# Attention stage: GpSimd multiplies one of four value rows, and its gathers are issued behind both sums of a pair

## The reference

```
gather = seg_id[:, :, None] - offsets            # 4 rows per token
scores = jnp.einsum('bhqd,bhqkd->bhqk', qh, k_sel) * SCALE
probs = jax.nn.softmax(scores, axis=-1)
out = jnp.einsum('bhqk,bhqkd->bhqd', probs, v_sel)
x = x + out @ Wo.T
x = x + ffn(layernorm(x))                        # peaks over the whole tensor
```

## Time and profile before

| | us |
|---|---|
| median of three runs | 2597.03 |
| profiled execution, its own time | 2596.16 |
| its span, first to last instruction | 2594.1 |
| attention stage in it, about | 121 to 735 |
| VectorE busy in the span | 1948.7 (75%) |
| TensorE busy in the span | 2023.5 (78%) |
| GpSimd busy in the span | 420.4 (16%) |

### The profile page before, as it was taken

The page is one execution under the profiler, slowest core; times in us unless marked ns, Lnnn a source line. Parts: engine busy times, 40 slices in busy tenths (PEclk is TensorE's granted clock), DMA queues, the critical chain, the costliest instruction groups (busy, mean ns, idle before and its releaser), DMA issues. The chain is left out here.

```text
span 2594.1 us, 26958 instructions
## 1 busy us (share of the span) xinstructions
PE 2023.5 (78%) x9560; PEld 948.2 (37%) x9560; DVE 1948.7 (75%) x1548; ACT 1518.1 (59%) x1507; POOL 420.4 (16%) x342
## 2 busy tenths in 40 slices
PE   4278888888659999999799999992000089999999
PEld 1134444444324444444344444441000034444444
DVE  8689999999824434532488888887999899877782
ACT  2536666666532322322466666666999898777770
POOL 0257676676600000000000000000000000000000
PEclk9589999999979999999899999996555589999999
DMA  7588888888344855732488888886777565555551
GB/s 267 208 366 322 331 317 331 323 314 332 126 162 163 245 195 176 248 130 114 187 285 287 290 287 286 290 278 270 277 274 275 197 239 211 218 221 228 228 204 65
DMA packets 142136, 633.62 MB, mean 244 GB/s; under 512 B 11616, under 2 KB 12128, under 8 KB 101856
## 3 DMA queue, kind: packets, MB, share of 16 engines
q1 hardware_dynamic: 132080, 495.61, 53.7%
q0 software_dynamic: 9216, 134.22, 13.4%
q10 hardware_dynamic: 752, 2.62, 0.3%
HBM read 453.23 MB, written 179.18 MB: 244 GB/s over the span
## 5 line engine op out<-in xcount | busy, mean ns | idle before, releaser
L1421 PE MATMUL fo_py<-kept_down,kept_gate 128*128 128x512 f16 x1536 | 459.0, 381 | 318.6 <-DVE kept_up L1402 318.6
L1182 PE MATMUL up_pp<-up_ah,kept_up 128*128 128x512 f16 x1536 | 459.0, 380 | 18.0 <-DVE up_al L1110 18.0
L1033 PE MATMUL ga_pp<-ga_ah,kept_gate 128*128 128x512 f16 x1536 | 458.3, 380 | 18.0 <-DVE ga_al L939 18.0
L1421 PEld LDWEIGHTS fo_py<-kept_down,kept_gate 128*128 128x128 f16 x1536 | 150.7, 98 | 501.5 <-DVE kept_up L1402 319.1
L979 DVE TENSOR_REDUCE kept_gate_peak<-ga_raw 128x1 f32<-128x2048 f32 x48 | 109.7, 2286 | 296.9 <-ACT ga_raw L1019 296.9
L1421 PE MATMUL fo_py<-kept_down,kept_up 128*128 128x512 f16 x768 | 292.1, 380 | 0.0
L1182 PE MATMUL up_pp<-up_al,kept_up 128*128 128x512 f16 x768 | 292.1, 380 | 0.0
L1033 PE MATMUL ga_pp<-ga_al,kept_gate 128*128 128x512 f16 x768 | 291.8, 380 | 0.0
L1019 ACT ACTIVATE ga_raw<-ga_pp 128x1024 f32<-128x1024 f32 x96 | 98.0, 1023 | 316.3 <-PE ga_pp L1033 316.3
L687 POOL TENSOR_TENSOR at_kv_rows<-at_kv_rows 128x1024 f32<-128x1024 f32 x64 | 215.0, 3360 | 158.0 <-DVE at_kv_rows L623 156.9
L1182 PEld LDWEIGHTS up_pp<-up_ah,kept_up 128*128 128x128 f16 x1536 | 150.7, 98 | 201.0 <-DVE up_al L1110 18.5
(11 more groups left out here) (194 smaller groups left out, 3565.2 us busy)
## 6 DMA issues: line engine op xcount, KB each, us to landing
gate_scratch<-ga_raw SPq DMA_DIRECT2D x48, 1024.0 KB, 4.9
up_gin<-gate_scratch SPq DMA_DIRECT2D x48, 1024.0 KB, 9.2
up_scratch<-up_raw SPq DMA_DIRECT2D x48, 1024.0 KB, 4.9
pp_ui<-up_scratch SPq DMA_DIRECT2D x48, 1024.0 KB, 5.6
fo_ui<-up_scratch SPq DMA_DIRECT2D x48, 1024.0 KB, 9.2
gate_integers<-up_gq SPq DMA_DIRECT2D x48, 512.0 KB, 9.7
pp_gq<-gate_integers SPq DMA_DIRECT2D x48, 512.0 KB, 3.6
fo_gi<-gate_integers SPq DMA_DIRECT2D x48, 512.0 KB, 7.3
```

The lines of the kernel that those rows point to most:

```text
L1033: mm = nc.tensor.matmul(pp[k % 4][:, h, :], wt[w][:, c, f:f + P], a[:, b % 2, :, c, :], start=(q == 0), stop=(q == len(todo) - 1))
L1182: mm = nc.tensor.matmul(bank[:, h, :], wt[w][:, c, f:f + P], a[:, u % 2, :, c, :], start=(q == 0), stop=(q == len(todo) - 1))
L1421: mm = nc.tensor.matmul(py[(u * SUB + t) % 8][:, :], a[u % 2][:, f, t * P:(t + 1) * P], wt[w][:, f, :], start=(q == 0 and i == 0), stop=(q ...
```

## The change

- `weigh` on VectorE covers the first three value rows; the fourth is left to GpSimd.
- `add_up` on GpSimd waits for the gathered rows, for the probabilities and for both tiles of the pair to be weighed, multiplies the fourth value row in place by its probabilities (128 x 512), and makes the two sums as before.
- The gathers of both tiles are issued behind the sums of both, in a function of their own, and the norm follows them.
- VectorE waits, before it writes the probabilities of a pair, until GpSimd has multiplied the rows of the pair before.

```
 def weigh(t):
-    values = kv[:, t % KR, :, D:2 * D].rearrange("p w (h e) -> p w h e", h=H)
-    nc.vector.tensor_tensor(values, values, pr[:, t % 2].unsqueeze(3).to_broadcast([P, W, H, HD]),
+    values = kv[:, t % KR, 0:W - 1, D:2 * D].rearrange("p w (h e) -> p w h e", h=H)
+    nc.vector.tensor_tensor(values, values, pr[:, t % 2, 0:W - 1].unsqueeze(3).to_broadcast([P, W - 1, H, HD]),
                             ALU.mult).then_inc(m["pv"], 1)
...
                         dve.wait_ge(m["inv"], s_ + 1)
+                        need(dve, m["last"], a)
                         nc.vector.tensor_tensor(pr[:, :, :, :], ex[:, :, :, :], inv[:, :, :].unsqueeze(2)...
...
 def add_up(t):
+    last = kv[:, t % KR, W - 1, D:2 * D].rearrange("p (h e) -> p h e", h=H)
     lower, upper = kv[:, t % KR, 0:2, D:2 * D], kv[:, t % KR, 2:4, D:2 * D]
-    pool.wait_ge(m["pv"], t + 1)
+    pool.wait_ge(rows_in[t % KR], 16 * (t // KR + 1))
+    pool.wait_ge(m["pr"], t // 2 + 1)
+    pool.wait_ge(m["pv"], t // 2 * 2 + 2)
+    nc.gpsimd.tensor_tensor(last, last, pr[:, t % 2, W - 1].unsqueeze(2).to_broadcast([P, H, HD]),
+                            ALU.mult).then_inc(m["last"], 1)
+    pool.wait_ge(m["last"], t + 1)
     nc.gpsimd.tensor_tensor(lower, lower, upper, ALU.add).then_inc(m["half"], 1)
...
                             ALU.add).then_inc(m["att"], 1)
+
+def gather_next(t):
     pool.wait_ge(m["att"], t + 1)
     gather(t + KR)
...
 if pair(s_ - 1):
     add_up(2 * s_ - 2)
     add_up(2 * s_ - 1)
+    gather_next(2 * s_ - 2)
+    gather_next(2 * s_ - 1)
 if pair(s_ - 3):
     norm(s_ - 3)
```

More of the change, by code:

```diff
@@ L469, in attention @@
         rows_in = [s.sem(f"rows_in{i}") for i in range(KR)]
-        m = s.sems("xn xT xhi xrest xlo q prod raw sc top ds ex tot inv pr pv half att aT ahi arest alo o x1 "
+        m = s.sems("xn xT xhi xrest xlo q prod raw sc top ds ex tot inv pr pv last half att aT ahi arest alo o x1 "
                    "nmean ssq sqe root rstd norm hn hT hT_sb peak consts reduced")
```

## The result

The changed kernel takes 2614.67 us (median of 7 runs, 2606.55 to 2616.15), the kernel before 2597.03 us in runs beside it (7 runs). The ratio is 1.0065 with a 95% interval of 1.005 to 1.0079: slower by 0.65%, where 2593.5 us had been forecast and the range ended at 2609. The profiled execution took 2616.02 us, with a span of 2613.9; that is 19.9 us more than the profiled one of before, and 18.8 of them are there when attention ends (GpSimd's last reduction of the stage starts at 753.75 and not at 734.96).

The account below looks back on a forecast made before the run. VectorE, busy 118.55 of 120 us in attention, was taken to bound the kernel. -34.1 + 20.5 + 5.6 + 1.5 + 3.0 = -3.5 us gave 2592.7 us, 2593.5 beside the median; the 8-in-10 range was 2567 to 2609.

Parts of the forecast that it names:

- What bounds the kernel, and the saving: Attention stage: VectorE sets the pace; weighing three value rows of four saves 1.06 us a slot, 34.1 us in all.
- The price of the multiplication: GpSimd's new multiplication of the fourth value row: 1.28 us, taken from the second addition, bounded by 0.29 and 2.37.
- the hold at sc: VectorE's score scaling waits for GpSimd's second sum, ending at 10.57 and not 9.91: 0.66 us a slot, 20.5 us.
- The prediction's own rate: Hold of VectorE's score scaling: each 0.1 us less of a multiplication counts twice a slot, 6.2 us.
- The catch of the norm: GpSimd: the norm's last instruction is held until VectorE's first weighing ends at 15.87, done at about 16.0.
- rival B: Norm not let in between the two weighings; hn at 17.7, VectorE idle 2.0 us at tot; about 2616 us; chance 0.10.
- The step that failed: VectorE's wait for the late exponential, plus 0.1 us at the second weighing: 0.2 us a slot, 5.6 us, ends 0 and 0.4.
- Steps at no cost: Gathers issued 6.8 and 3.0 us later, SP's queue, and VectorE's wait for the fourth row before pr: nothing lost.
- The waits on more semaphores: Two more on GpSimd and one on VectorE: 0.05 us a slot together, 1.5 us, ends 0 and 0.16.
- The end of the stage: Last pair, no gather: GpSimd's second sum over at 10.42 and not 7.45 behind the slot's first product; 3.0 us lost.
- The sum: Whole kernel: -34.1 + 20.5 + 5.6 + 1.5 + 3.0 = -3.5 us, 2592.7 us, or 2593.5 beside the median.

Follow-up runs that it names:

- the first experiment: The changed kernel with GpSimd's norm issued behind the two sums and ahead of the two gathers: 2572.76 us, ratio 0.9899 against the kernel before.

## Why the prediction was wrong

- *What bounds the kernel, and the saving.* Right: VectorE paces the stage; 34.1 us forecast, 34.2 measured.
- *The price of the multiplication.* Taken from the second sum, 1.28 us; measured 1.05. The step that was mis-sized by it is the hold at sc, 20.5 us in the sum: the second sum is over at 9.90 us behind T and not at 10.42, sc loses about 0.15 us in most slots and not 0.66, 6.0 us in all. The prediction's own rate (6.2 us for each 0.1 us less) gives 20.5 - 14.3 = 6.2 us, so the mechanism was right, and the gathers inside the tiles' work show it at 0.81 us a slot.
- *The catch of the norm.* Right in place and kind: the shift instruction held to the end of the first weighing (forecast done at 16.0, measured 421.81 - 406.40 = 15.4, earlier by the cheaper multiplication). It got in between the two weighings, and the pair of them lost nothing by it (3.43 us with the catch and without, 0.1 us more forecast), so rival B's reason ("is not let in between") was wrong, though its path (hn, query, exponential, tot) and its shape (every second slot) were what happened. That B's price, about 2616 us, lies beside the measured 2614.67 is luck: it came from an hn at 17.7 and a wait of 2.0 us at full clock, and from the forecast's 20.5 us at sc.
- *The step that failed*: "That is up to 0.3 us lost, nothing in a slot in which the norm got through before the weighing. I take 0.2 us a slot for both, 28 slots: 5.6 us". Measured: 40.9 us. The 7.75 us from hn to the next query were read from a trace in which TensorE ran at full clock. In that trace it waited 1.9 us ahead of this projection in the middle of the stage; after the change it waits 4.6 us, the clock falls to half in the slot shown, the projection takes 5.1 us and not 2.6, and hn to query is 10.31. The prediction worked out each step of this chain and left out that the step behind a longer idle stretch can run at the lower clock. The added matmuls take the clock away as a cause and leave 0.37 us behind a catch; the exponential moved forward takes the path away, and some of the idle time with it, and leaves 0.4 to 0.5; the norm moved forward takes the cause away and leaves nothing. The trace of before already had the row that was missed, behind the last pair:

```profile
428.87 0.60 PE L723 MATMUL at_psO<-kept_wo,at_ahi 128*128 128x512 f16 x2 [1.92 <-ACT at_alo L536]
428.87:431.47 2.60, 2.60 (x13) 1.23 (x14) 2.60 (x2) 1.85 (x5) 0.41 (x1) 1.00 1.01 424
711.44 1.03 PE L723 MATMUL at_psO<-kept_wo,at_ahi 128*128 128x512 f16 x2 [4.53 <-ACT at_alo L536]
711.44:715.50 4.06, 4.06 (x12) 1.59 (x13) 0.00 (x0) 1.85 (x5) 0.00 (x0) 0.63 0.32 117
```

Behind 1.92 us of idleness the twelve matmuls took 2.6 us at full clock, and behind 4.53 us they took 4.1 us at a mean of 0.63.

- *Steps at no cost.* Right: the gathers' lateness and VectorE's wait for the fourth row cost nothing. The waits on more semaphores on VectorE, 1.5 us in the sum together with GpSimd's, do not show: pr starts as soon after the reciprocal as before. The end of the stage is 3.2 us against 3.0 forecast, which is partly luck: the second sum ends 0.5 us earlier behind T than the 10.42 from which the 3.0 was made.
- *The sum.* -34.2 + 6.0 + 40.9 + 3.2 = +15.9 us against -3.5. Two large terms were off, sc 14.5 us too dear and tot 35.3 too cheap, and the 1.5 us for semaphores did not show; the range did not reach the second because its bound (0.4 us a slot) was that of a path at constant clock.

## What to carry to other kernels

Work moved to an engine that is not the bottleneck also moves everything that is queued behind it there: put what others wait for (here four instructions of 0.2 to 0.7 us) ahead of what nobody waits for (here gathers with 12 us of slack). Where two engines exclude each other, look at which instruction meets which, and at the chain behind the one that loses, rather than at the sum of the holds. And when a step of TensorE is made to start later, price it at the clock that it may find. A row that shows it at full clock behind 1.9 us of idleness says nothing of the same step behind 4.6, and the length of the wait alone does not settle it: with the exponential moved forward, projections behind 2.2 us ran at full clock in some slots and at a mean of about 0.62 in others.

## What was not expected of the hardware

- A GpSimd tensor-tensor instruction of 128 x 512 takes 1.05 us with a broadcast second operand (16 numbers for 512 elements) and 1.27 us with two full ones, product or sum.
- Adding 2.6 us of matmuls a slot whose result is overwritten made the kernel 32 us faster than the changed one, and adding a wait on the engine that sets the pace 29 us faster.
- The Trainium skill (SBUF — State Buffer, section SBUF: two separate sides) calls the pair of ports that VectorE and GpSimd share an exclusive lock for the full instruction. The runs agree for instructions from 128 x 128 upwards on VectorE and 128 x 512 on GpSimd (ds ended 0.16 us after the sum that held it), and a 128 x 2 instruction of GpSimd that starts 0.15 us into a 1.75 us weighing is held until it ends. The norm's power instruction, 0.72 us on 128 x 2, held up nothing (ds at 0.29 us beside it in the first experiment), though it is itself held by a weighing: 2.25 us in the fourth slot of the changed kernel.
